# Layer norm statistics on rows in a two-layer vision tower: transposes and per-row statistics in place of products with a constant matrix

## The reference

```python
def _layernorm(x, axis=-1, eps=1e-05):
    m = jnp.mean(x, axis=axis, keepdims=True)
    v = jnp.var(x, axis=axis, keepdims=True)
    return (x - m) / jnp.sqrt(v + eps)
```

## Time and profile before

| | us |
|---|---|
| median of 3 runs | 309.04 |
| lowest and highest | 308.05, 309.98 |
| the profiled execution, first to last instruction (its span) | 308.5 |
| TensorE busy in it | 301.2 |
| VectorE, ScalarE, GpSimd busy | 188.7, 186.6, 157.2 |

### The profile page before, as it was taken

How to read it: one execution, slowest core, us unless ns; L and a number is a source line. 1 busy time by engine, 2 the same in 40 slices (tenths; PEclk the granted TensorE clock), 3 DMA queues, 4 the chain that set the end, 5 groups by cost and what they waited for, 6 DMA issues and landing times.

```text
span 308.5 us, 7389 instructions
## 1 busy us (share of the span) xinstructions
PE 301.2 (98%) x3082; PEld 278.5 (90%) x3082; DVE 188.7 (61%) x367; ACT 186.6 (60%) x326; POOL 157.2 (51%) x144
## 2 busy tenths in 40 slices
PE   8999999999999999999999999999999999999895
PEld 7877789999998999989999999999999999987673
DVE  2685255656546778467828775664738496746862
ACT  4486337765536793357698566757567464568651
POOL 6042425863525131747868495867685886100332
PEclk9999999999999999999999999999999999999999
DMA  7969353454302331669584838384757643000002
GB/s 257 405 156 232 70 130 125 138 182 147 115 19 87 119 104 42 212 193 279 188 249 137 263 117 290 107 281 149 272 170 216 212 165 88 21 2 3 0 0 83
DMA packets 32432, 46.49 MB, mean 151 GB/s; under 512 B 6965, under 2 KB 18837, under 8 KB 32394
## 3 DMA queue, kind: packets, MB, share of 16 engines
q1 hardware_dynamic: 29994, 42.16, 43.6%
q0 software_dynamic: 960, 2.43, 2.4%
q10 hardware_dynamic: 1440, 1.38, 1.5%
HBM read 38.22 MB, written 5.71 MB: 142 GB/s over the span
## 4 chain that ended last, share of the span: by engine, by line
PE 91%; DVE 4%; ACT 3%; issue 1%; ACTq 0%; POOL 0%; DVEq 0%; POOLq 0%
PE ps L1638 22%; PE ps L1640 22%; PE ps L1639 21%; PE ps L1994 6%; PE ps L1823 3%; PE ps L1789 3%; PE ps L1660 3%; PE ps L1653 2%; PE ps L1774 2%; PE ps L1668 2%; PE ps L1646 1%; PE ps L1904 1%; PE ps L1868 1%; DVE xn_split L1412 1%; ACT w_hi L809 1%
## 5 line engine op out<-in xcount | busy, mean ns | idle before, releaser
L1638 PE MATMUL ps<-c_region,w_hi 128*128 128x224 f32 (+2 forms) x304 | 88.2, 290 | 0.7 <-DVE c_region L1082 0.7
L1640 PE MATMUL ps<-c_region,w_lo 128*128 128x224 f32 (+2 forms) x304 | 85.3, 281 | 0.0
L1639 PE MATMUL ps<-c_region,w_hi 128*128 128x224 f32 (+2 forms) x304 | 85.2, 280 | 0.0
L560 POOL TENSOR_TENSOR w_lo<-w_stage,w_hi 128x512 fp32r<-128x512 f32 x30 | 48.5, 1635 | 31.1 <-ACT w_hi L809 31.0
L1638 PEld LDWEIGHTS ps<-c_region,w_hi 128*128 128x128 f32 x304 | 58.1, 191 | 1.8 <-DVE c_region L1082 1.2
L1639 PEld LDWEIGHTS ps<-c_region,w_hi 128*128 128x128 f32 x304 | 58.1, 191 | 0.3
L1640 PEld LDWEIGHTS ps<-c_region,w_lo 128*128 128x128 f32 x304 | 58.0, 191 | 0.0
L809 ACT ACTIVATE w_hi<-w_stage 128x1024 fp32r<-128x1024 f32 (+1 forms) x42 | 49.7, 1196 | 2.6 <-DVE v_region L1484 2.6
L1082 DVE TENSOR_TENSOR c_region<-s_region,c_region 128x448 fp32r<-128x448 f32 (+1 forms) x44 | 37.3, 848 | 17.5 <-ACT c_region L936 11.6
L567 POOL TENSOR_TENSOR w_lo<-w_stage,w_hi 128x512 fp32r<-128x512 f32 x28 | 37.9, 1384 | 8.3 <-ACT w_hi L809 8.3
L1638 PE MATMUL ps<-xn_split,w_hi 128*128 128x296 f32 x128 | 40.2, 314 | 0.5 <-DVE xn_split L1082 0.4
(11 more groups left out here) (183 smaller groups left out, 573.4 us busy)
## 6 DMA issues: line engine op xcount, KB each, us to landing
w_stage<-in_w_gate SPq DMA_DIRECT2D x17, 512.0 KB, 4.2
w_stage<-in_w_up SPq DMA_DIRECT2D x17, 512.0 KB, 4.5
w_stage<-in_w_down SPq DMA_DIRECT2D x7, 1024.0 KB
expert_rows<-blank_rows SPq DMA_DIRECT2D x4, 448.0 KB, 3.5
v_region<-in_blocks SPq DMA_DIRECT2D x6, 272.0 KB, 4.0
w_stage<-in_w_down SPq DMA_DIRECT2D x3, 512.0 KB
v_region<-expert_rows SPq DMA_DIRECT2D x1, 1344.0 KB, 8.3
expert_out<-v_region ACTq DMA_DIRECT2D x6, 224.0 KB, 4.4
```

The costliest lines, as they stand in the source:

```text
L560: w = g.tensor_tensor(wl[:, r], ws[:, r], wh[:, r].bitcast(F32), ALU.subtract)
L1638: mm(o, a_h, b_h, start=start, stop=False)
L1639: mm(o, a_h, b_l, start=False, stop=False)
L1640: return mm(o, a_l, b_h, start=False, stop=stop)
```

## The change

The sums over features are made on rows. `turn_in(L, c)` transposes the half of `hT` with six transposes into three PSUM tiles (128, 128 and 40 tokens on partitions, 256 features in columns). On VectorE `sums` takes the statistics of each tile (`bn_stats` and `bn_aggr`), ScalarE's `root` works on three columns, `normal` subtracts and scales each row tile with two per-row scalars from PSUM into SBUF, and `turn_back(L, c)` turns the rows back with six transposes. `take_back`, `take_halves` or `take_spread` copy the result to `xnf`; `high` and `low` read it from PSUM. `square`, the matrix `ones` and the centred copy go.

The expert stage takes its row tiles straight from `normal(1, c)`, so `turn_tokens` goes. Its token tiles now follow the halves: `TT` = 6 tiles (128, 128, 40 for each half) in place of five, `TA` = 3 of them in the first half in place of 2. The partial products of the merge go; logits, spreads, scatters and fetches have six tiles. `shared_down_low(0)` moves from VectorE to GpSimd. The 128x128 identity is loaded earlier.

```diff
-            def centre(L, c):
-                dve.wait_ge(s["ln_mean"], 2 * L + c + 1)
...
-                    v.tensor_tensor(chunk(xc[:], c), chunk(hT[:], c), pat(mean_bank(L, c), 0, [0, KD], [1, NC]),
-                                    ALU.subtract).then_inc(s["ln_xc"], 1)
+            def sums(L, c):
+
+                for i in range(TA):
+                    n, j = tokens(i), TA * nth(L, c) + i
+                    dve.wait_ge(s["ln_turn"], C * nth(L, c) + i // 2 + 1)
+                    v.bn_stats(bn[0:n, j * 6:(j + 1) * 6], row_bank(L, c, i)[0:n, :]).then_inc(s["ln_bn"], 1)
+                for i in range(TA):
+                    n, j = tokens(i), TA * nth(L, c) + i
+                    dve.wait_ge(s["ln_bn"], j + 1)
+                    v.bn_aggr(mv[0:n, 2 * j:2 * j + 2], bn[0:n, j * 6:(j + 1) * 6]).then_inc(s["ln_mv"], 1)
 
             def normal(L, c):
...
+                dve.wait_ge(s["ln_rs"], nth(L, c) + 1)
+                for i in range(TA):
+                    n, j = tokens(i), TA * nth(L, c) + i
+                    v.tensor_scalar(row_tile(L, c, i), row_bank(L, c, i)[0:n, :], mv[0:n, 2 * j:2 * j + 1],
+                                    rstd[0:n, j:j + 1], ALU.subtract, ALU.mult).then_inc(s["ln_row"], 1)
+
+            def take_back(L, c):
+
+                dve.wait_ge(s["ln_back"], nth(L, c) + 1)
+                v.tensor_copy(chunk(xnf[:], c, NT), turned_back(L, c)).then_inc(s["ln_xn"], 1)
...
+            def turn_in(L, c):
+
+                pe.wait_ge(s["h_ready"], 4 * L + 2 * c + KD)
+                for i in range(TA):
+                    for k in range(KD):
+                        o = k * N + c * NC + i * P
+                        w = nc.tensor.transpose(row_bank(L, c, i)[0:tokens(i), k * P:(k + 1) * P],
+                                                hT[:, o:o + tokens(i)], ident)
+                    if i >= 1:
+                        w.then_inc(s["ln_turn"], 1)
+
+            def turn_back(L, c):
+
+                apart = ROWS_IN[L, c] != ROWS_BACK[L, c]
+                for i in range(TA):
+                    n = tokens(i)
+                    pe.wait_ge(s["ln_row"], TA * nth(L, c) + (i + 1 if apart else TA))
+                    for k in range(KD):
+                        w = nc.tensor.transpose(bank(ROWS_BACK[L, c] + k, n, i * P),
+                                                row_tile(L, c, i)[:, k * P:(k + 1) * P], ident[0:n, 0:n])
+                w.then_inc(s["ln_back"], 1)
...
                 if u == 2:
+                    turn_back(1, 1)
                     pe.wait_ge(s["dn0_lo"], 1)
-                    pe.wait_ge(s["xt_ok"], 1)
+                    pe.wait_ge(s["rows_set"], 1)
...
-                    pe.wait_ge(s["mixed"], TT if c else 3)
+                    pe.wait_ge(s["mixed"], TA * (c + 1))
...
-            centre(2, 1)
+            sums(2, 1)
             add_state(0, 0, state(0, 0, inject(0, 0)))
             normal(2, 1)
             add_state(0, 1, state(0, 1, inject(0, 1)))
+            take_halves(1)
             scan10 = state(1, 0, inject(1, 0))
-            centre(3, 0)
+            sums(3, 0)
...
+            take_spread(0)
+            sums(3, 1)
             mix(0, 1, 0)
             mix(0, 0, 0)
+            normal(3, 1)
             mix(0, 1, 1)
             mix(0, 0, 1)
-            normal_spread(1)
+            take_spread(1)
```

More of the change, by code:

```diff
@@ L344, in qk_bank, with nth, row_bank, row_tile @@
         def qk_bank(n):
[L346 to L368, removed]
+            return 4 if n == 0 else 6
+        ROWS_IN = {(0, 0): 0, (0, 1): 4, (1, 0): 0, (1, 1): 6, (2, 0): 4, (2, 1): 6, (3, 0): 0, (3, 1): 2}
+        ROWS_BACK = {(0, 0): 2, (0, 1): 6, (1, 0): 2, (1, 1): 6, (2, 0): 4, (2, 1): 6, (3, 0): 4, (3, 1): 6}
+        def nth(L, c):
+            return C * L + c
+        def row_bank(L, c, i):
+            return bank(ROWS_IN[L, c] + i // 2, D, i % 2 * D)
+        def row_tile(L, c, i):
+            o = (TA * c + i) * D
+            return (xt_f if L == 1 else xr)[0:tokens(i), o:o + D]
+        def turned_back(L, c):
+            return pat(bank(ROWS_BACK[L, c]), 0, [512, KD], [1, NC])
         def rows_of(a, c, m):
@@ L1504, in _ @@
                 weigh(4)
-                centre(2, 0)
                 back_mul(3)
+                sums(2, 0)
+                weigh(5)
                 back_low(2)
@@ L1649, in _ @@
             keep_clock(9)
-            def mean(L, c):
-                for k in range(KD):
-                    pe.wait_ge(s["h_ready"], 4 * L + 2 * c + (k + 1 if (L, c) in FINE else KD))
-                    w = mm(mean_bank(L, c), ones[:], hT[:, k * N + c * NC:k * N + (c + 1) * NC],
-                           start=(k == 0), stop=(k == KD - 1))
-                w.then_inc(s["ln_mean"], 1)
-            def variance(L, c):
-                for k in range(KD):
-                    pe.wait_ge(s["ln_sq"], centred(L, c) + (k if (L, c) in FINE else 0) + 1)
-                    w = mm(var_bank(L, c), ones[:], sq[:, k * N + c * NC:k * N + (c + 1) * NC],
-                           start=(k == 0), stop=(k == KD - 1))
-                w.then_inc(s["ln_var"], 1)
+            def turn_in(L, c):
[16 more added lines that the diff above has]
+                w.then_inc(s["ln_back"], 1)
             def embed(k, c):
@@ L1914, in _ @@
             gate_up(0, 0)
-            mean(1, 1)
-            turn_tokens(0)
+            turn_in(1, 1)
+            logits(0, TA, 2)
             gate_up(0, 1)
             positions(0, TA, 2)
-            variance(1, 1)
             for u in range(2, FRONT):
@@ L2142, in _ @@
                 back_gate_up(3)
-                mean(2, 0)
+                turn_in(2, 0)
                 back_down(0)
                 back_down(1)
-                merge(1, variance_and_down)
+                merge(1, down_and_turn)
                 back_down(3)
@@ L2170, in _ @@
                 back()
-                mean(2, 0)
-                variance(2, 0)
+                turn_in(2, 0)
+                turn_back(2, 0)
                 last_layer()
```

286 lines of the change are left out of this document (128 added, 158 removed).

## The result

The changed kernel takes **318.88 us** (median of 4 runs, 317.65 to 319.25) against 308.75 (4 runs, 308.05 to 309.98): 1.033 times as long, 95% interval 1.029 to 1.037. Slower was forecast, by half as much: 314.0, with a range up to 318.2, so the time lies above the range. The profiled execution spans 316.8 us.

A forecast was written before the change was run, and what follows sets the result against it. TensorE, 98% busy, was taken as the bound, except the last 16 us, set by norm latency. Arriving 0.25 us early, then +5.25 at the end, gave +5.0: span 313.5, plus 0.5, 314.0 us; range 309.8 to 318.2.

The forecast's parts named there:

- layers 0 and 1: about 0: First two layers: gains and added VectorE work sum to about 0, reaching the last norms some 0.25 us early.
- the price of transposes with 40 rows: Turns back, spreads and merges on TensorE: a record of 40 or 88 columns costs 0.095 us; six turns back 0.62.
- the walk: Step-by-step timing of the kernel's end: last 48 records start at 297.8 against 292.55, time 314.0 us; chance 0.47.
- What bounds the kernel: Whole kernel: TensorE, 98% busy, but the last 16 us are set by the latency of the last norms.
- TensorE's share: TensorE's work: 17.8 us less, 11.2 more, a gain of 6.6 us if nothing else waits.
- VectorE's share: Each norm half on VectorE: 3.7 us where it was 1.5, with statistics 0.42 and scalings 0.47 each.
- the scan-like rival: VectorE's statistics cost like a scan, 0.69 us for 256 columns: +3.3, 317.3 us; chance 0.11.
- The forecast positions' wait: Layer 1's front: positions wait for the ranking of experts from 107.45 to 108.85.
- The merge and layer 2's first half: Before the first gate: second merge waits 0.75 us, first gate starts at 275.05 against 274.73 before.
- The end: Layer 2's second half and layer 3: first gate at 275.05, last 48 records at 297.8, against 274.73 and 292.55.
- That rival: Kernel's end: clock falls in the waits, last products start at 1.2 GHz, losing 2.1 us: 316.1 us; chance 0.11.
- The rule about the clock: Kernel's end: if transposes don't count as busy work, TensorE does nothing that counts from 288.3 to 293.15.

The follow-up runs named there:

- the third profile: The kernel before, unchanged, profiled once more on the chip of the later runs: 308.44 us (ratio 0.9996), span 306.7 us.

## Why the prediction was half right

The direction was right and the size was half of what came. The step that failed most is "layers 0 and 1: about 0", which measured 2.3 us; the next are the price of transposes with 40 rows and the clock that the walk kept at 1.00.

- **What bounds the kernel**: right. The loss is latency: TensorE's load is no bound where it rests on VectorE's rows.
- **TensorE's share** (-6.6): the turn in is sized right (0.65), but the turn back took 0.77 without waits where 0.62 was forecast, 1.2 us for eight, and a group of six in the spreads and merges took 1.03 where 0.65 was expected, 1.5 us for four. Both hold tiles of 40 rows, which the prediction priced like the others. The half rate adds 3.4 (4.95 for 3.15, 3.56 for 1.95). Against the third profile the busy time rose by 1.5 where it was to fall by 6.6; the 2 us that are left were not broken down.
- **VectorE's share**: statistics 0.42 as taken (the scan-like rival at 0.69 falls), three aggregations 0.29 instead of 0.5, scalings 0.53 instead of 0.47, three of them 1.35 to 1.44 instead of 1.27.
- **Layers 0 and 1 ("about 0")**: the step that failed most. The changed front is 2.1 us longer, and with attention and start the kernel is 2.2 late at the first expert turn where 0.25 early was forecast. The forecast positions' wait until 108.85 ended at 110.52. Its sum let VectorE's ranking run undisturbed beside the residue "now GpSimd's and hidden there": that piece stretched one comparison by 1.1 us. But removing the stretch only moved the wait. I balanced the front wait by wait, where the chain as a whole sets it: the row numbers came 8.5 us behind the first gate product (5.1 before, the ranking ahead of it), of it 7.4 to 7.7 VectorE's own list, and with the stretch gone still 8.2 to 8.4, since waits for ScalarE's root or TensorE's logits come up. Why these come late was not tested. I also let TensorE keep a lead of 1.25 us at the first gate product, which attention's pauses and a wait of 0.23 took down to under half.
- **The merge and layer 2's first half** (+0.57 from the last expert on): 2.19. Of the 1.6 between them, 1.5 is what the four groups took over their forecast. The wait of 0.75 ahead of the second merge came as said, 0.72; another 0.43 stood ahead of the turn back.
- **The end (+4.93 from first gate to last 48 records)**: 5.60. The right total hides two errors: with the clock held it is 3.7, so the walk was 1.2 too dear, in part by its sums (1.3 us a half where 1.6 was taken, three halves); and the clock, which the walk kept at 1.00, cost 1.9. That rival was priced at 2.1, with chance 0.11; the price came near by luck, since it was half of a stretch at the kernel's start, where the profile's rows show a granted clock of 1.00.
- **The rule about the clock**: the clock fell, but not because transposes don't count. The Trainium skill's sentence ("TensorE: Matmul & The Clock Gate", Part 4: PE-mode transpose) doesn't hold for these fp32 transposes: with them in the waits the granted clock read 1.00 from 284 to 292, as with idle products. What I passed over was the idle in my own walk, some 5 us of it in the last layer (5.17 measured). I also misread as gaps of 0.7 to 1 us: TensorE is idle there for 0.70 us in all.
- **The baseline**: one profile stood for the kernel before. It was 1.8 us longer than the third profile, in the start, the front, the experts and the last 48 records (by 0.5, 0.4, 0.7 and 0.4). By spans the loss looked like 8.3 us; it is 10.1.

In all, of the 5.1 us between forecast and measured loss: 2.5 are layers 0 and 1, 1.6 the merge with its short tiles, 0.7 the end, net of two errors; 0.3 is rounding between profiles and medians.

## What to carry to other kernels

Where engines alternate with little slack, measure the whole chain between two fixed points before counting waits one by one: here 1.1 us less in one item moved the end of the chain by 0.26. A saving in a busy engine is worth nothing where the data it waits for arrives later, and the idle that it gains can halve its clock just ahead of the work that sets the end, in some executions and not in others. Profile the baseline more than once before a change of 1% is read out of its marks, since one execution here was 1.8 us off.

## What the hardware showed that I had not expected

- A VectorE operation with two inputs from the on-chip memory took 1.39 us instead of 0.31 while a GpSimd subtraction of 512 columns ran (107.19 to 108.48), and 0.31 with that moved.
- One change more from weights of 128 rows to weights of 40 costs TensorE 0.27 us in a group of six transposes; 128 to 80 and back cost nothing that shows (starts 0.11 and 0.07 us apart).
- Waits of 1.3 to 2.15 us on TensorE were followed by work at half the clock in some profiles and not in others with the same waits: in the end the first fall came in four of six, the second in three of six. With transposes or idle products in those waits neither came, in one profile each.
- A tile of 40 rows costs VectorE as much as one of 128: 0.525 against 0.530 us for the scaling, 0.404 against 0.420 for the statistics.
